# Two-layer adjacency attention, fp32 by halves: layer 1's query-key weight product placed at the head of the program, piece by piece

## What is computed

```python
h = jnp.maximum(_layernorm(x, axis=-1), 0.0)
x = x + _L0_gnn_ref(h, adj, Wq, bq, Wk, bk, Wv, bv)     # 8 heads of 64, masked softmax
h = jnp.maximum(_layernorm(x, axis=-1), 0.0)
x = x + _L1_gnn_ref(h, adj, Wq, Wk, Wv)
# layer 1, per graph:
q = einsum('bnd,ed->bne', h, Wq); k = einsum('bnd,ed->bne', h, Wk); v = einsum('bnd,ed->bne', h, Wv)
rel = adj.T * (q @ k.T); rel = rel / norm(rel, axis=2); out = rel @ v
```

## Time and profile before

| what | us |
|---|---|
| median of 3 runs (2459.55, 2465.02, 2463.25) | 2463.25 |
| the profiled execution's own time | 2464.18 |
| its span | 2462.4 |
| PE busy | 2396.4 (97%) |
| ACT busy | 1686.4 (68%) |
| DVE busy | 1450.8 (59%) |
| POOL busy | 1298.9 (53%) |
| in the chain that ended last: PE | 84% |

### The profile page before, as it was taken

How to read it: one execution, slowest core, us unless ns; L and a number is a source line. 1 busy time by engine, 2 the same in 40 slices (tenths; PEclk the granted TensorE clock), 3 DMA queues, 4 the chain that set the end, 5 groups by cost and what they waited for, 6 DMA issues and landing times.

```text
span 2462.4 us, 53549 instructions
## 1 busy us (share of the span) xinstructions
PE 2396.4 (97%) x19252; PEld 1301.3 (53%) x19252; DVE 1450.8 (59%) x4435; ACT 1686.4 (68%) x4111; POOL 1298.9 (53%) x1159
## 2 busy tenths in 40 slices
PE   6999999999999999999999999999999999999986
PEld 3455555555555555555555555555555555555543
DVE  5555666555666556666555665555665556666543
ACT  5667777667676677776677766776776776766762
POOL 3555555555555555555555555555555555555541
PEclk9999999999999999999999999999999999999998
DMA  7566666676676566666665766665755666765652
GB/s 207 111 133 135 131 147 138 123 140 130 137 148 129 120 137 129 153 138 130 126 138 129 151 133 126 140 138 126 150 138 123 140 135 132 150 136 120 124 111 65
DMA packets 938841, 329.14 MB, mean 134 GB/s; under 512 B 885968, under 2 KB 886224, under 8 KB 938576
## 3 DMA queue, kind: packets, MB, share of 16 engines
q1 hardware_dynamic: 935744, 322.31, 63.1%
q10 hardware_dynamic: 2832, 3.41, 0.4%
HBM read 73.93 MB, written 33.55 MB: 44 GB/s over the span
## 4 chain that ended last, share of the span: by engine, by line
PE 84%; DMA 4%; DVE 4%; ACT 3%; POOL 3%; issue 2%; SPq 1%; ACTq 0%; DVEq 0%
PE B L686 70%; PE S L759 7%; PE O L686 6%; DMA probs_t<-halves 3%; ACT probs L481 1%; DVE stats L545 1%; POOL halves L375 1%; ACT h L421 1%; POOL v L371 1%; DMA h1t<-h_halves 1%; PE B L716 1%; ACT halves L489 0%; POOL h_halves L361 0%; ACT h_halves L428 0%; DVE masked L620 0%
## 5 line engine op out<-in xcount | busy, mean ns | idle before, releaser
L375 POOL TENSOR_TENSOR halves<-probs,halves 128x512 f16<-128x512 f32 x512 | 596.5, 1167 | 532.8 <-ACT halves L489 532.6
L481 ACT ACTIVATE probs<-masked,neg_max 128x256 f32<-128x256 f32 x1024 | 508.4, 498 | 222.5 <-DVE neg_max L620 221.8
L620 DVE CUSTOM_DVE_ANT_0 masked<-S,mask 128x256 f32<-128x256 f32 x1024 | 386.4, 417 | 129.4 <-PE S L759 129.3
L361 POOL TENSOR_TENSOR h_halves<-h,h_halves 128x512 f16<-128x512 f32 x256 | 295.0, 1158 | 150.4 <-ACT h_halves L428 150.4
L686 PE MATMUL B<-wv,h0t 128*128 128x512 f16 x1536 | 355.0, 381 | 19.4 <-DMA h0t<-h_halves 19.4
L686 PE MATMUL B<-wvt,h1t 128*128 128x512 f16 x1536 | 349.5, 381 | 12.6 <-DMA h1t<-h_halves 12.6
L686 PE MATMUL B<-h0t,wq 128*128 128x512 f16 x1536 | 352.8, 379 | 1.0 <-DVE k_st L605 0.5
L686 PE MATMUL B<-h0t,wk 128*128 128x512 f16 x1536 | 352.5, 379 | 0.0
L686 PE MATMUL B<-h1t,wm 128*128 128x512 f16 x1536 | 346.9, 379 | 0.0
L489 ACT ACTIVATE halves<-probs 128x512 f16<-128x512 f32 x512 | 322.5, 630 | 16.2
L686 PEld LDWEIGHTS O<-v,probs_t 128*128 128x128 f16 x6144 | 247.7, 98 | 143.0 <-DMA probs_t<-halves 23.8
(11 more groups left out here) (70 smaller groups left out, 2941.8 us busy)
## 6 DMA issues: line engine op xcount, KB each, us to landing
x_in<-in_x_dram SPq DMA_DIRECT2D x128, 256.0 KB, 3.2
x_res<-in_x_dram SPq DMA_DIRECT2D x128, 256.0 KB, 3.8
out_dram<-result SPq DMA_DIRECT2D x128, 256.0 KB, 2.5
probs_t<-halves SPq DMA_TRANSPOSE x512, 2.9
h0t<-h_halves SPq DMA_TRANSPOSE x128, 3.2
h1t<-h_halves SPq DMA_TRANSPOSE x128, 3.3
rv<-in_L_gnn_Wv_dram ACTq DMA_DIRECT2D x2, 512.0 KB, 6.0
rq<-in_L_gnn_Wq_dram ACTq DMA_DIRECT2D x2, 512.0 KB, 7.6
```

The source lines that it names most:

```text
L361: nc.gpsimd.tensor_tensor(h_halves[:, n, 1, :], h[:, n % 2, :], h_halves[:, n, 0, :], ALU.subtract).then_inc(h_low[layer], 1)
L375: nc.gpsimd.tensor_tensor(halves[:, n % RING, 1, :], probs[:, n % 2, :, :].rearrange("p t n -> p (t n)"), halves[:, n % RING, 0, :], ALU.s ...
L481: ins = nc.scalar.activation(probs[:, n % 2, i, :], masked[:, n % 2, i, :], ACT.Exp, bias=neg_max[:, n % 2, i:i + 1], scale=-1.0, accum_ou ...
L620: ins = nc.vector.tensor_tensor_reduce(out=masked[:, n % 2, i, :], in0=S[n % 4][:, i, :], in1=mask[:, i, :], scale=SCORE, scalar=BIG, op0= ...
```

## The change

1. PE forms wm before anything else: for each k of four, when rows k of Wq1 and Wk1 have landed, four matmuls, one into each of the scores' banks S0 to S3. The setup_rq steps leave PE's plan.
2. ACT and DVE write the halves of wm in slots 2 to 5 of turn 0, before the first scores (which now wait for them), instead of slots 21 to 24.
3. The weights of layer 1 have staging places of their own: Wq1 in rq, Wk1 in x_res[1], Wv1 in h1t. Layer 0's Wq is staged in v[1] and Wk in x_res[0]. The waits of SP for the low halves before loading are gone.
4. ACT issues eight loads of 256 KB (Wq1 and Wk1, one k each) ahead of layer 0's six; only the first two don't wait for the second x tile. The biases' loads go from ACT to SP, between the x tiles and adj.
5. ACT's head does h and its halves for all four tiles before it touches the weights.
6. The hand-written plan is written as a timetable. Walked through engine by engine, the orders are those of before, apart from the moved setup_rq steps.

```diff
+    OPENING = {("rq", 0): 2, ("rq", 1): 3, ("rq", 2): 4, ("rq", 3): 5}
...
+        others += [(slot, 5, "setup_rq", n) for (kind, n), slot in OPENING.items()]
...
-        stage = [as_weight(rv), as_weight(rq), x_res[:, 1, :, :]]
+        stage = [as_weight(rv[:, :, :, :]), as_weight(v[:, 1, :, :, :]), x_res[:, 0, :, :]]
+        stage_q, stage_k = as_weight(rq[:, :, :, :]), x_res[:, 1, :, :]
+        stage_v = as_weight(h1t[:, :, :, :])
@@ sync
             for t in range(TILES):
                 sp.dma_start(x_in[:, t, :], xv[0][:, t, :]).then_inc(x_loaded[t], 16)
+            sp.dma_start(bq[:, :], bq0.rearrange("(m p) -> p m", p=P),
+                         allow_slow_non_contiguous=True).then_inc(small_loaded, 16)
+            sp.dma_start(bk[:, :], bk0.rearrange("(m p) -> p m", p=P),
+                         allow_slow_non_contiguous=True).then_inc(small_loaded, 16)
+            sp.dma_start(bv[:, :], bv0.partition_broadcast(P)).then_inc(small_loaded, 16)
             sp.dma_start(adj_in, adj.rearrange("(t p) n -> p t n", p=P)).then_inc(adj_loaded, 16)
             for n in range(TILES):
                 turn_h(0, n, 0)
-            for n, w in enumerate((wv1, wq1, wk1)):
-                sp.wait_ge(w_low, 2 * n + 2)
-                sp.dma_start(stage[n], w.rearrange("(t p) n -> p t n", p=P)).then_inc(w_loaded[n], 16)
+            sp.dma_start(stage_v, wv1.rearrange("(t p) n -> p t n", p=P)).then_inc(wvt_loaded, 16)
@@ scalar
-            act.wait_ge(x_loaded[1], 16)
+            for k in range(KT):
+                if k == 1:
+                    act.wait_ge(x_loaded[1], 16)
+                for buffer, w in ((stage_q, wq1), (stage_k, wk1)):
+                    rows = w.rearrange("(t p) n -> p t n", p=P)
+                    act.dma_start(buffer[:, k, :], rows[:, k, :]).then_inc(wm_loaded[k], 16)
             for n, w in enumerate((wv0, wq0, wk0)):
                 rows = w.rearrange("(t p) n -> p t n", p=P)
                 for part in range(2):
                     ts = slice(2 * part, 2 * part + 2)
                     act.dma_start(stage[n][:, ts, :], rows[:, ts, :]).then_inc(w_part[n][part], 16)
-            act.dma_start(bq[:, :], bq0.rearrange("(m p) -> p m", p=P),
-                          allow_slow_non_contiguous=True).then_inc(small_loaded, 16)
-            act.dma_start(bk[:, :], bk0.rearrange("(m p) -> p m", p=P),
-                          allow_slow_non_contiguous=True).then_inc(small_loaded, 16)
-            act.dma_start(bv[:, :], bv0.partition_broadcast(P)).then_inc(small_loaded, 16)
...
-            for n in range(2):
-                ln_apply(0, x_in, n, 0, h_low[0], 0)
-            for n in range(2):
-                h_high_half(0, n, 0, h_turned[0][n], 0)
-            weight_high(0, wv, WS)
-            for n in range(2, 4):
-                ln_apply(0, x_in, n, 0, h_low[0], 0)
-            for n in range(2, 4):
-                h_high_half(0, n, 0, h_turned[0][n], 0)
+            for first in (0, 2):
+                for n in (first, first + 1):
+                    ln_apply(0, x_in, n, 0, h_low[0], 0)
+                for n in (first, first + 1):
+                    h_high_half(0, n, 0, h_turned[0][n], 0)
+            weight_high(0, wv, WS)
@@ tensor
+            for k in range(KT):
+                pe.wait_ge(wm_loaded[k], 32)
+                for n in range(KT):
+                    ins = nc.tensor.matmul(setup_bank("setup_rq", n, 0), stage_q[:, k, col(n)], stage_k[:, k, :],
+                                           start=(k == 0), stop=(k == KT - 1))
+                    if k == KT - 1:
+                        ins.then_inc(setup_product, 1)
...
                 elif kind == "scores":
...
+                    if p == 0 and n == 0:
+                        pe.wait_ge(setup_done, len(OPENING))
```

More of the change, by code:

```diff
@@ L92, in tensor_slot @@
[L92 to L106, removed]
-        steps += on(at, [(slot - 1, "mask", n) for slot, n in SECOND])
-        steps += on(at, [(slot + 1, "inverse", m) for m, slot in enumerate(ENDED)])
-        steps += BESIDE.get(at, [])
-        for slot, n in BY_UNIT:
-            steps += on(at, [(slot, "exp", n), (slot, "split", n)])
-        return steps + LOADS.get(at, [])
@@ L114, in adjacency_attention_two_layers @@
-    TENSOR_PLAN = [step for at in range(PERIOD) for step in tensor_slot(at)]
-    PLAN = [step for at in range(PERIOD) for step in other_slot(at)]
-    TURNS = PAIRS + 2
-    PROJECT = [(kind, n) for kind, n, _ in SLOTS if kind in ("q", "k", "v")]
-    RELATE = [(kind, n) for back in (1, 2) for kind, n, b in SLOTS if b == back]
+    LAYER0 = {"x_in": [-25, -25, -24, -24], "ln0_stats": [-14, -14, -13, -13], "ln0_power": [-13],
+              "ln0_scale": [-10], "ln0_apply": [-8, -8, -5, -2], "ln0_split": [-8, -8, -5, -2],
+              "x_res": [13, 13, 14, 14], "residual": [17, 23, 28, 34]}
@@ new lines, in adjacency_attention_two_layers, with timetable @@
+    LAYER1 = {"ln1_stats": [35, 35, 36, 36], "ln1_power": [36], "ln1_scale": [38], "ln1_apply": [38] * TILES,
+              "ln1_split": [38] * TILES, "squares": [53, 56], "rel_scale": [53, 56], "rel_split": [54, 57]}
+    OPENING = {("rq", 0): 2, ("rq", 1): 3, ("rq", 2): 4, ("rq", 3): 5}
+    def timetable():
+        tensor = [(slot, 0, "scores", m) for m, slot in enumerate(SCORED)]
+        tensor += [(slot, 1, kind, n) for (kind, n), slot in PRODUCT_AT.items()]
+        tensor += [(slot, 2, "pv", n) for n, slot in enumerate(MULTIPLIED)]
+        others = [(slot + 1, 0, "norm", m) for m, slot in enumerate(MULTIPLIED[3::4])]
+        others += [(slot + 1, 1 if kind == "v" else 3, kind, n) for (kind, n), slot in PRODUCT_AT.items()]
+        others += [(slot + 2, 5, "inverse", m) for m, slot in enumerate(MASKED[1::2])]
+        for j, slot in enumerate(MASKED):
+            others += [(slot, 2, "mask", 2 * j), (slot, 4, "mask", 2 * j + 1)]
+            others += [(slot + e, 7, kind, 2 * j + e) for e in range(2) for kind in ("exp", "split")]
+        others += [(slot, 5, "setup_rq", n) for (kind, n), slot in OPENING.items()]
+        for layer in (LAYER0, LAYER1):
+            for n in range(TILES):
+                others += [(at[n], 8 if kind[0] == "x" else 6, kind, n) for kind, at in layer.items() if n < len(at)]
+        return tensor, others
@@ new lines, in in_order @@
+    def in_order(steps):
+        order = []
+        for p in range(-1, PAIRS):
+            for i, (slot, place, kind, n) in enumerate(steps):
+                if p >= 0:
+                    if not (p == 0 and slot < 0) and not (p > 0 and kind == "setup_rq"):
+                        order.append((PERIOD * p + slot, place, p, i, kind, n))
+                elif (kind, n) in SETUP and kind != "rq":
+                    order.append((PERIOD * p + slot, place, p, i, "setup_" + kind, n))
+        return [(kind, n, p) for _, _, p, _, kind, n in sorted(order)]
@@ L122, in adjacency_attention_two_layers @@
     REL_LAST = RELATE.index(("rel", 1)) + 1
-    SETUP = [st for st in RELATE if st[0] in ("rq", "rv") or st == ("rel", 0)]
+    SETUP = list(OPENING) + [st for st in RELATE if st[0] == "rv" or st == ("rel", 0)]
     NSETUP = len(SETUP)
-    def pairs(plan):
-        for turn in range(TURNS):
-            for kind, n, back in plan:
-                if kind in ("rv", "rq", "rel") and turn - back == -1 and (kind, n) in SETUP:
-                    yield "setup_" + kind, n, turn - back
-                elif 0 <= turn - back < PAIRS:
-                    yield kind, n, turn - back
-    KINDS = ("q", "k", "v", "rv", "rq", "rel", "out", "setup_rv", "setup_rq", "setup_rel")
-    PRODUCTS = [step for step in pairs(TENSOR_PLAN) if step[0] in KINDS]
+    TENSOR_PLAN, PLAN = [in_order(steps) for steps in timetable()]
+    KINDS = ("q", "k", "v", "rv", "rq", "rel", "out", "setup_rv", "setup_rel")
+    PRODUCTS = [step for step in TENSOR_PLAN if step[0] in KINDS]
     BANKS = 3
@@ L366, in _ @@
                 h_low_half(0, n, 0)
-            for kind, n, p in pairs(PLAN):
+            for kind, n, p in PLAN:
                 if kind == "v":
```

66 lines of the change are left out of this document (25 added, 41 removed), and 13 rows, old and new, of tables (BESIDE, PRODUCT_AT, SLOTS).

## The result

In 22 runs of each kernel the changed one took 2459.37 us at the median (2457.14 to 2466.18), the one before 2463.89 (2459.55 to 2470.5): a ratio of 0.9985, with 95% between 0.9978 and 0.9991, or 3.7 us less (2.2 to 5.4). The gain is read from the ratio; the two medians by themselves are 4.5 us apart. The forecast was 2465.6, no change, in a range from 2460.5. The profiled execution of the changed kernel, 2466.18 us (span 2464.4, mean clock 0.991), was the slowest of the 22, so its own time says nothing; its stretches do.

The account below looks back on a forecast made before the run. PE was taken to bound the steady turns and the setup_rq stretch, ACT's queue the head. 1.45 + 0.7 + 1.2 - 1.0 = +2.35 us on the median 2463.25 gave 2465.6 us, range 2460.5 to 2471.5.

Parts of the forecast that it names:

- Head: Start of the kernel up to scores 0: later first h, later k 0 and later wm halves, +1.45, +0.7 and +1.2 us.
- first h 1.45 later: ACT's queue at the start: tile 1 at 5.1, then twelve issues of 7.7 us, put first h at 14.1, not 12.65.
- S: Start of ACT's first h, from which the head's times are counted: 12.65 us before, forecast 14.1, ends 11.4 to 20.5.
- the term of 0.7: Head: with h done before the weights, k 0 starts at S + 15.5 instead of S + 14.8, 0.7 us later.
- Scores 0 held by wm's halves for 1.2: Head's end: last wm half ends 9.0 us after k 0's start, against 7.86 before; 1.2 us later, ends 0.2 and 2.
- Middle: Removed setup_rq stretch: pv 8 and k 3 come 3.1 us earlier, less 2.1 for slow clock; 1.0 gained, ends 3.1 and -1.1.
- Equal distances from there on: After scores 3: the two kernels differ only by a constant; any other difference behind 120 us would make the prediction wrong.
- Clock stays up: Rival, middle: three pv keep PE at 2.4 GHz, so the full 3.1 us is gained; 2463.5 us, chance 0.17.
- v 0 slow: Rival, head: v 0 starts at the slow clock after a 3.0 us pause, +2.5 us; 2468.1 us, chance 0.13.
- Slow queue: Rival, head: all twelve ACT issues cost 1.10 us and tile 1 lands at 6.0; +8.8 us, 2472.0 us, chance 0.17.
- Paid in full: Rival, middle: the removed 13.9 us of PE pay in full and the head is free; 2449.4 us, chance 0.05.
- Not hidden: Rival, head: product stays at 1.2 GHz, takes 27.8 us, ends 8.5 behind v 0's time; 2474.1 us, chance 0.03.

Follow-up runs that it names:

- old_order: Changed kernel with ACT's high half of Wv again ahead of h 2 and 3, as in the kernel before: 2464.24 us, ratio 0.9987 to before.
- mid_product: Changed kernel with the product wm put back into its middle slots, loads and head order as changed: 2469.86 us, ratio 1.0015 to before.
- fill: Changed kernel with 28 extra matmuls, results unused, in PE's idle time of the middle: 2462.81 us, ratio 0.9982 to before.
- after_again: Changed kernel run again unchanged, second profiled execution: own time 2465.9 us; timed 2464.53 us, ratio 0.9986 to before.
- one_piece: Changed kernel with three of the product's four pieces left out, loads and waits kept: 2463.87 us, ratio 0.9982 to before.
- sp_loads: Changed kernel with the eight Wq1 and Wk1 loads issued by SP behind the x tiles instead of by ACT: 2463.26 us, ratio 0.9989 to before.
- after_look1: Changed kernel, nothing altered, third profiled execution, untimed: own time 2456.1 us.
- after_look3: Changed kernel, nothing altered, fifth profiled execution, untimed: own time 2462.1 us.
- after: Changed kernel, its first profiled execution: own time 2466.2 us.
- after_look2: Changed kernel, nothing altered, fourth profiled execution, untimed: own time 2458.3 us.

## Why the prediction was wrong

From +2.35 forecast to -3.7 measured it is 6.0 us. The head gave 1.3 of them, the stretch from scores 0 to scores 2, for which the sum had no term, 0.35, the middle 2.4, and some 2.0 lie behind scores 3 and stay open.

**Head, +3.35 predicted, +2.06 on average.** The terms: first h 1.45 later, measured 0.7. Three of twelve issues were to cost 1.10; none did. All took 0.34 to 0.55, together 5.9 us in place of 7.7; only the wait for tile 1 was longer, to 6.12 in place of 5.1. k 0 at S + 15.5: it started at S + 15.63, right, but the term of 0.7 in it isn't the price of the new order: with the order of before, old_order has k 0 at S + 16.03 (29.31 less 13.28). What holds it there is the last turn of h, for which the prediction took S + 11.7. It landed at S + 12.84 in the change (26.19, q 0 started at 26.39), since the first two turns took 5.8 us in place of 3.2 and held SP's queue. That the loads beside them make them slow is likely by the times; no run isolates it. Scores 0 held by wm's halves for 1.2: they began 8.1 behind k 0 (predicted 9.05; 7.86 before), so 0.2. The pieces went in the order predicted, but they don't queue up: by the timeline of DVE, changed kernel, the last one waits for v 1's product, through v_sum and two operations of ACT:

```profile
34.36 0.69 DVE L598 TENSOR_TENSOR v_sum<-B,bv 128x512 f32<-128x512 f32 x1
36.23 0.69 DVE L583 SCALAR_TENSOR_TENSOR wm<-S,wm 128x512 f16<-128x512 f32 x1 [1.18 <-ACT wm L442]
```

The low end that the prediction kept (0.2) was the right one. That the product is hidden, that it starts at the slow clock and that v 0 is fast behind it were right; the pause before v 0 was 0.8 us, not 3.0, mostly because the first rows landed 1.4 later than assumed. That mid_product's head came out at +3.4 is no confirmation of my sum, which had v 0 fast.

**Middle, -1.0 predicted, -3.4 measured.** This is the step that failed. Its form held: pv 8 waited for the turn of unit 8 and not for line 716's work, PE stood idle, the clock fell to 0.50, k 3 took 3.89 from its start to the next (predicted 4.4; the row's 4.05 includes the overlap), and the loss at the slow clock was 1.4 to 1.7 by fill (predicted 2.1). The size of the first term was wrong: "pv 8 and k 3 can come 3.1 us earlier and no more". That bound rested on one landing of 4.7 us in one execution. It landed in 2.9 to 3.2 us in four profiles of the change; the 4.7 held the standstill. In the change's first profile pv 8 started 11.4 us behind scores 2, against 16.5 before (76.72 - 60.21): 5.1 earlier, not 3.1. Of the difference 1.5 is the landing, and the rest is POOL, which waited for x 0.66 less (its addition starts 1.65 behind scores 2 in place of 2.31). What is late next was named rightly; its length was taken over as if it were the transfer's own. Where the standstill did hit the turn (after_again) the gain was 1.4, near the forecast's 1.0, with k 3 slow throughout (5.31). That the standstill sets the landing rests on these profiles side by side and on the count in the steady part; no run moved it by itself.

**Behind 120 us.** "Equal distances from there on" fell. I had counted the steady part as fixed; it has 9 to 23 us of stalls that change from run to run, and the profiled pair alone would have had the sign wrong (2466.18 against 2464.18).

**The rivals.** Clock stays up: refuted, the row shows 0.50. v 0 slow: refuted for the change, whose pause before v 0 was 0.8 us and not 3.0; true of mid_product and one_piece. Slow queue: refuted, no issue took more than 0.55 us, where the forecast had three at 1.10. Paid in full: refuted by mid_product. What the prediction took from the earlier trace rows, that a group of scores keeps its full-clock 1.48 us behind a pause of 2.58, was one execution; in the four other profiles of before the same group took 2.4 to 2.7. Not hidden: refuted by the gap before v 0, though at 0.8 us it was nearer than I gave it, and sp_loads tips it. The Trainium skill, TensorE: Matmul & The Clock Gate, section on HAM oscillation, was right that a waiting PE between bursts is throttled; the trace agrees with 0.50, and it changed only the size of the gain.

**What remains open** is the part of the measured 3.7 us above the 1.7: some 2 us in the stalls or in their scatter.

## What to carry to other kernels

When work leaves the path, what is late next sets the gain, and if that is a transfer, its landing must be taken apart before it serves as a bound: of these 4.7 us some 1.5 came from a standstill of all DMA that need not come along. An engine that would be idle at the start is a good place for work of 16 us, doubly when it takes the slow stretch of the clock upon itself; the same move leaves a hole where the work was, and the clock falls there. At gains of 0.1% compare distances between fixed instructions of several profiles, not the spans.

## What the hardware showed that I had not expected

- Twelve issues on ACT's queue, of 4.7 MB together, cost 0.34 to 0.55 us each; before, with 3.1 MB, some cost 1.10. On the same queue in sp_loads, beside SP's own issues, six took 4.2 us.
- PE's stalls recur near the same places of the program in both kernels (450, 484, 545, 842, 1156, 1380, 1513, 1677 us), but not in every execution. A packet of the instruction queue q8 stands by the standstill near 71 us in all ten profiles, and by 351 of 360 standstills of the steady part. That loading instructions causes them, and with them PE's stalls, is likely by this; no run isolates it. Three turns in ten meet such a packet, and PE waits for few of them (8 to 16 waits for probs_t in a profile).
- Behind the gap of 2.57 us that both kernels have the earlier trace rows the clock may fall at once, a little later, or not at all. From the start of these scores to the next step behind q 1 a profile at full clock has 4.0 us: the first of before, after_again and after_look1. The seven others have 5.3 to 5.7. In four of before and in after_look3 the scores themselves took 2.4 to 2.7 us in place of 1.48, and q 1 2.80 to 3.46; in after and after_look2 the scores took 1.6 to 1.7 and q 1 4.29 and 4.20 in place of 2.75. Timeline of PE, first profile of the change:

```profile
109.29 1.59 PE L749 MATMUL S<-k_st,q_st 64*128 64x256 f16 x24 [2.57 <-DVE k_st L591]
110.81 4.29 PE L672 MATMUL B<-h0t,wq 128*128 128x512 f16 x12
```
